# Gated delta rule in a two-layer decoder: the unit's output formed with features on partitions, its norm applied at the residual addition

## The reference, cut to what matters

```python
S = S * alpha_t; kv = k_t @ S; S = S + outer(k_t, (v_t - kv) * beta_t); o_t = q_t @ S
...
var = jnp.mean(jnp.square(o), axis=-1, keepdims=True)
o = o * lax.rsqrt(var + EPS) * norm_w
o = o * (z * jax.nn.sigmoid(z))
out = jnp.einsum('btv,hv->bth', o.reshape(b_, t_, VAL_DIM), out_w)
```

## Time and profile before

| | us |
|---|---|
| median of 3 runs | 1917.11 (1915.36 to 1921.35) |
| the profiled execution | 1916.25 |
| its span on the core | 1914.9 |
| PE busy | 1837.5 (96% of the span) |
| DVE busy | 1221.8 |
| POOL, ACT busy | 696.3, 681.2 |

### The profile page before, as it was taken

One profiled execution on the slowest core, in us unless ns is written; L12 is line 12 of the kernel. 1 busy time (PEld: TensorE's weight loads), 2 busy tenths in 40 slices (PEclk: granted clock), 3 DMA queues, 4 the chain that ended last, 5 costly groups with the idle time before them and its releaser, 6 DMA issues.

```text
span 1914.9 us, 39982 instructions
## 1 busy us (share of the span) xinstructions
PE 1837.5 (96%) x15048; PEld 1331.2 (70%) x15048; DVE 1221.8 (64%) x3371; ACT 681.2 (36%) x1755; POOL 696.3 (36%) x726
## 2 busy tenths in 40 slices
PE   7799999999899999999999999999999999999999
PEld 4466766776676666666445766666659979889698
DVE  6878888878766776777766766767655334234332
ACT  4223333333334555555000355565642211121211
POOL 4634443444215676666000166666634000000000
PEclk9889999999999999999999999999999999999999
DMA  5111101110103010010000000100030000000000
GB/s 186 29 22 21 31 15 28 23 25 14 23 15 124 25 37 25 26 37 20 1 1 1 10 20 20 29 20 20 20 144 34 1 10 1 10 1 1 10 1 10
DMA packets 94591, 52.22 MB, mean 27 GB/s; under 512 B 77256, under 2 KB 86336, under 8 KB 93632
## 3 DMA queue, kind: packets, MB, share of 16 engines
q1 hardware_dynamic: 94400, 49.65, 9.8%
HBM read 44.18 MB, written 5.45 MB: 26 GB/s over the span
## 4 chain that ended last, share of the span: by engine, by line
PE 68%; issue 2%; DVE 2%; ACT 1%; POOL 1%; DVEq 0%; ACTq 0%; POOLq 0%
PE ps L2534 18%; PE ps L1517 6%; PE ps L2406 5%; PE ps L2065 5%; PE ps L1539 5%; PE ps L1555 4%; PE ps L1594 4%; PE ps L1573 4%; PE ps L2612 3%; PE ps L1660 2%; PE ps L1526 2%; PE ps L1605 1%; PE ps L1581 1%; PE ps L1642 1%; PE ps L556 1%
## 5 line engine op out<-in xcount | busy, mean ns | idle before, releaser
L1978 POOL TENSOR_TENSOR h_w<-h_w 125x336 int32<-125x336 int32 x384 | 335.9, 904 | 210.8 <-ACT h_w L1759 210.7
L1863 DVE CUSTOM_DVE_ANT_0 h_w<-ps,h_w 112x375 f32<-112x375 f32 x512 | 263.4, 544 | 0.8 <-issue 0.5
L903 DVE SCALAR_TENSOR_TENSOR big_b<-ps,taps,big_b 128x444 f32<-128x444 f32 (+2 forms) x288 | 193.9, 673 | 34.3 <-ACT big_b L790 15.6
L1759 ACT ACTIVATE h_w<-ps 125x336 f32<-125x336 f32 x512 | 197.7, 468 | 21.7 <-PE ps L1539 21.7
L272 POOL TENSOR_TENSOR rstd<-var_eps,minus_half 112x4 f32<-112x4 f32 x12 | 12.2, 1015 | 408.0 <-DVE var_eps L259 408.0
L1539 PEld LDWEIGHTS ps<-h_w 32*125 32x125 f32 x3072 | 96.0, 183 | 62.3 <-issue 61.5
L1539 PE MATMUL ps<-h_w 32*125 32x112 f32 x3072 | 118.0, 282 | 8.0 <-DVE h_w L1863 5.6
L1872 DVE TENSOR_TENSOR h_w<-h_w,ps 128x112 f32<-128x112 f32 x128 | 34.7, 271 | 141.6 <-PE ps L1526 141.6
L1517 PE MATMUL ps<-h_w 32*112 32x375 f32 x1024 | 121.1, 519 | 0.8 <-DVE h_w L1863 0.8
L2065 PE MATMUL ps<-expert_w,big_a 128*112 128x512 f32 x256 | 114.1, 597 | 0.0
L556 PE MATMUL ps<-h_w,w 128*128 128x448 f32 x256 | 109.6, 552 | 4.6 <-ACT h_w L812 4.6
(11 more groups left out here) (357 smaller groups left out, 3852.7 us busy)
## 6 DMA issues: line engine op xcount, KB each, us to landing
h_w<-in_h SPq DMA_DIRECT2D x2, 4096.0 KB, 16.8
kq_w<-in_ctxT SPq DMA_DIRECT2D x16, 375.0 KB, 3.2
h_w<-in_ctxT SPq DMA_DIRECT2D x16, 375.0 KB, 3.3
h_w<-in_mask SPq DMA_DIRECT2D x16, 164.1 KB, 3.3
kq_w<-in_kq_w SPq DMA_DIRECT2D x8, 256.0 KB, 3.4
w<-in_vz_w SPq DMA_DIRECT2D x8, 256.0 KB, 3.5
blocks<-h_w SPq DMA_DIRECT2D x128, 12.2 KB
expert_w<-in_expert_w SPq DMA_DIRECT2D x1, 2048.0 KB
```

Source lines behind the costliest of these rows:

```text
L903: dve.scalar_tensor_tensor(p3(dst)[:, :, i:], p3(ps[:, bank, 0:GT])[:, :, 0:T - i], k.taps[:, h, n, TAPS - 1 - i:TAPS - i], p3(dst)[:, :, ...
L1759: act.activation(k.PTx[(4 * Q + r) % RING], ps[0:CK, turned_bank(Q, r), 0:NC * T], ACT.Exp).then_inc(s["exp"], 1)
L1863: dve.tensor_tensor_reduce(k.masked[r % 2], ps[0:T, score_bank(Q, r), 0:S2], k.mask_add[n % 2], -1.0, 3.0e38, ALU.add, ALU.min, k.neg_max[ ...
L1978: pool.tensor_tensor(P.bitcast(I32), P.bitcast(I32), k.mask_I[n % 2], ALU.mult).then_inc(s["weights"], 1)
```

## The change

O is formed transposed (features on partitions) by swapping the operands, so the transposes and their wait go. ACT squares all of it in one instruction; PE sums the squares of each token by four products of a 128x112 stationary operand with a single column that holds 1/128; ACT copies those means and adds 1e-6; POOL takes the power -1/2; DVE multiplies by norm weight and gate straight from bank 6; the root is applied in the addition to x, for which four instructions of 112x256 take the place of two of 112x512. Bank 6 is now released by the squares and by the gated product.

```diff
         elif slot == 3:                      # keys(): logG on PE
             if a > AHEAD:
-                pe.wait_ge(s["On"], a - AHEAD)
+                pe.wait_ge(s["squares"], a - AHEAD)
+                pe.wait_ge(s["gated"], a - AHEAD)
...
         if u:                                # out_of(u) on PE
-            pe.wait_ge(s["On"], u)
-        for j in range(G):
-            ins = pe.matmul(ps[0:T, 6, j * DK:(j + 1) * DK], k.R[u % 2][:, j, :], k.W0[u % 2][:, j * DK:(j + 1) * DK],
-                            start=True, stop=True)
+            pe.wait_ge(s["squares"], u)
+            pe.wait_ge(s["gated"], u)
+        for j, c in enumerate(PER_SEQ):
+            ins = pe.matmul(ps[:, 6, c], k.W0[u % 2][:, j * DK:(j + 1) * DK], k.R[u % 2][:, j, :], start=True, stop=True)
...
         if slot == 2:                        # tail(u, slot) on PE
-            pe.wait_ge(s["On"], u + 1)
-            pe.wait_ge(s["sz"], min(u + 2, UNITS))
-            if is_late(u):
+            pe.wait_ge(s["squares"], u + 1)
+            if u:
                 pe.wait_ge(s["gdn_x"], u)
-            for j in range(G):
-                ins = pe.transpose(ps[:, 4, j * T:(j + 1) * T], k.On[:, j * DK:(j + 1) * DK], k.ident[0:T, 0:T])
-            ins.then_inc(s["oT"], 1)
+            for j, c in enumerate(PER_SEQ):
+                ins = pe.matmul(ps[0:T, 0, j:j + 1], k.squared[:, c], k.mean_col[:, :], start=True, stop=True)
+            ins.then_inc(s["mean"], 1)
         elif slot == 4:
             pe.wait_ge(s["gated"], u + 1)
+            pe.wait_ge(s["o_var"], u + 1)
+            pe.wait_ge(s["sz"], min(u + 2, UNITS))
...
         keys(a, 2)                           # steady loop on PE
-        if u:
-            tail(u - 1, 2)
         solve(u, "Y2")
...
         keys(a, 10)
+        tail(u, 2)
         solve(u + 1, "M")
...
-        tail(u - 1, 2)                       # late loop on PE, behind V
+        if u > UNITS - AHEAD:
+            tail(u - 1, 2)
...
     def squares(u):                          # ACT
         act.wait_ge(s["O"], u + 1)
-        for j in range(G):
-            ins = act.activation(k.On[:, j * DK:(j + 1) * DK], ps[0:T, 6, j * DK:(j + 1) * DK], ACT.Square,
-                                 accum_out=k.var_eps[:, j:j + 1])
-        ins.then_inc(s["squares"], 1)
+        if u:
+            act.wait_ge(s["mean"], u)
+        act.activation(k.squared, ps[:, 6, 0:GT], ACT.Square).then_inc(s["squares"], 1)
+
+    def mean(u):
+        act.wait_ge(s["mean"], u + 1)
+        if u:
+            act.wait_ge(s["o_rstd"], u)
+        act.activation(k.var_eps[:, :], ps[0:T, 0, 0:G], ACT.Copy, bias=1e-6).then_inc(s["o_var"], 1)
...
         values(u + 1, 8)                     # steady loop on ACT
+        mean(u)
         solve(u + 1, "R")
...
         more = is_unit(u + 1)                # late loop on ACT
+        if u > UNITS - AHEAD:
+            mean(u - 1)
         solve(u, "A")
...
-        if slot == 1:                        # tail(u, slot) on DVE
-            dve.wait_ge(s["squares"], u + 1)
-            dve.tensor_scalar(k.var_eps[:, :], k.var_eps[:, :], 1.0 / DK, 1e-6, ALU.mult, ALU.add).then_inc(s["o_var"], 1)
-        elif slot == 2:
-            dve.wait_ge(s["o_rstd"], u + 1)
-            dve.tensor_tensor(four(k.On), four(ps[0:T, 6, 0:G * DK]), k.rstd[:, :].unsqueeze(2).to_broadcast([T, G, DK]),
-                              ALU.mult).then_inc(s["On"], 1)
-        elif slot == 3:
-            dve.wait_ge(s["oT"], u + 1)
+        if slot == 3:
+            dve.wait_ge(s["squares"], u + 1)
...
-            dve.scalar_tensor_tensor(k.oT, ps[:, 4, 0:GT], k.norm_w[:, 0:1], k.sz[u % 2], ALU.mult, ALU.mult).then_inc(s["gated"], 1)
+            dve.scalar_tensor_tensor(k.oT, ps[:, 6, 0:GT], k.norm_w[:, 0:1], k.sz[u % 2], ALU.mult, ALU.mult).then_inc(s["gated"], 1)
         elif slot == 5:
             dve.wait_ge(s["out"], u + 1)
-            for n in range(G // 2):
-                xs = k.x[:, g * G + 2 * n:g * G + 2 * n + 2, :]
-                ins = dve.tensor_tensor(xs, xs, two(ps[0:T, out_banks(u)[n], :]), ALU.add)
+            dve.wait_ge(s["o_rstd"], u + 1)
+            for j in range(G):
+                xs = k.x[:, g * G + j, :]
+                ins = dve.scalar_tensor_tensor(xs, ps[0:T, out_banks(u)[j // 2], (j % 2) * D:(j % 2 + 1) * D], k.rstd[:, j:j + 1], xs,
+                                               ALU.mult, ALU.add)
...
     def root(u):                             # POOL
         pool.wait_ge(s["o_var"], u + 1)
+        if u:
+            pool.wait_ge(s["gdn_x"], u)
...
             sums(u + AHEAD)                  # steady loop on POOL
-            root(u - 1)
...
             fades(u + AHEAD + 1)
+        root(u)
```

More of the change, by code:

```diff
@@ L50 @@
 zeros proj_kq tap_kq conv_kq proj_vz tap_v conv_v cum kk tanh sz logG gamma gam kq N0 QG vtok W0
-nd_w0 nd_w1 ni_in c_in tri td_w pair_in pair off_w dn_in0 dn_in1 M_ps M R_ps R Y1 A Y2 less Y3 R_sum O squares o_var o_rstd On oT gated out gdn_x
+nd_w0 nd_w1 ni_in c_in tri td_w pair_in pair off_w dn_in0 dn_in1 M_ps M R_ps R Y1 A Y2 less Y3 R_sum O squares mean o_var o_rstd gated out gdn_x
 ctx0 ctx1 mask_in0 mask_in1 k_bias
@@ L148, in memory @@
     k.W0 = [spare[:, n * G * DK:(n + 1) * G * DK] for n in range(2)]
-    k.On = k.xn[:, 0:2, :].rearrange("p a b -> p (a b)")
+    k.squared = k.silu[:, 0, :]
+    k.mean_col = sb("mean_col", [128, 1])
     k.beta_decay = k.small[:, 0:8, :].rearrange("p a b -> p (a b)").rearrange("p (n h g j) -> p n h g j", n=2, g=NG, j=G)
@@ L692, in gdn_pe @@
     pe.wait_ge(s["c_ident"], 16)
+    pe.wait_ge(s["setup_pool"], 2)
     start_pe_turn(pe, k, s, 0)
@@ L773, in gdn_pe @@
     cross_head_pe(pe, k, s, 0, 3)
-    for slot in range(4):
-        tail(UNITS - 1, slot)
+    tail(UNITS - 1, 2)
     cross_head_pe(pe, k, s, 0, 2)
-    for slot in (4, 5):
-        tail(UNITS - 1, slot)
+    tail(UNITS - 1, 4)
 def gdn_act(act, k, s):
@@ L891, in gdn_act @@
     act.wait_ge(s["const"], 64)
-    for part in (1, 0, 2, 3, 4):
+    cross_head_act(act, k, s, 0, 1)
+    mean(UNITS - 1)
+    for part in (0, 2, 3, 4):
         cross_head_act(act, k, s, 0, part)
@@ L960, in tail @@
         g = u % NG
-        if slot == 1:
+        if slot == 3:
             dve.wait_ge(s["squares"], u + 1)
-            dve.tensor_scalar(k.var_eps[:, :], k.var_eps[:, :], 1.0 / DK, 1e-6, ALU.mult, ALU.add).then_inc(s["o_var"], 1)
-        elif slot == 2:
-            dve.wait_ge(s["o_rstd"], u + 1)
-            dve.tensor_tensor(four(k.On), four(ps[0:T, 6, 0:G * DK]), k.rstd[:, :].unsqueeze(2).to_broadcast([T, G, DK]),
-                              ALU.mult).then_inc(s["On"], 1)
-        elif slot == 3:
-            dve.wait_ge(s["oT"], u + 1)
-            if u == 0:
+            if u:
+                dve.wait_ge(s["out"], u)
+            else:
                 dve.wait_ge(s["setup_dve"], 1)
-            dve.scalar_tensor_tensor(k.oT, ps[:, 4, 0:GT], k.norm_w[:, 0:1], k.sz[u % 2], ALU.mult, ALU.mult).then_inc(s["gated"], 1)
+            dve.scalar_tensor_tensor(k.oT, ps[:, 6, 0:GT], k.norm_w[:, 0:1], k.sz[u % 2], ALU.mult, ALU.mult).then_inc(s["gated"], 1)
         elif slot == 5:
             dve.wait_ge(s["out"], u + 1)
-            for n in range(G // 2):
-                xs = k.x[:, g * G + 2 * n:g * G + 2 * n + 2, :]
-                if u == UNITS - 1 and n == 1:
+            dve.wait_ge(s["o_rstd"], u + 1)
+            for j in range(G):
+                xs = k.x[:, g * G + j, :]
+                if u == UNITS - 1 and j == 2:
                     dve.wait_ge(s["out"], u + 2)
-                ins = dve.tensor_tensor(xs, xs, two(ps[0:T, out_banks(u)[n], :]), ALU.add)
+                ins = dve.scalar_tensor_tensor(xs, ps[0:T, out_banks(u)[j // 2], (j % 2) * D:(j % 2 + 1) * D], k.rstd[:, j:j + 1], xs,
+                                               ALU.mult, ALU.add)
             ins.then_inc(s["gdn_x"], 1)
@@ L1020, in gdn_dve @@
         h4, h3, h2 = head_due(u, 4), head_due(u, 3), head_due(u, 2)
-        if u:
-            tail(u - 1, 1)
-            tail(u - 1, 2)
         if h3 is not None:
@@ L1078, in gdn_dve @@
     cross_head_dve(dve, k, s, 0, 1)
-    for slot in range(6):
+    for slot in (3, 5):
         if slot == 5:
@@ L1153, in gdn_pool @@
             fades(u + AHEAD + 1)
+        root(u)
     for u in range(UNITS - AHEAD, UNITS):
         h3, h2 = head_due(u, 3), head_due(u, 2)
-        root(u - 1)
+        if u > UNITS - AHEAD:
+            root(u - 1)
         if h2 is not None:
@@ L2844, in gpsimd_program @@
     pool.memset(k.minus_half[:, :], -0.5).then_inc(s["setup_pool"], 1)
+    pool.memset(k.mean_col[:, :], 1.0 / DK).then_inc(s["setup_pool"], 1)
     pool.wait_ge(s["setup_pool"], 1)
```

## The result

The changed kernel takes 1927.01 us (median of 5 runs, 1922.21 to 1928.30), the kernel before 1916.71 (5 runs). The ratio is 1.005 with a 95% interval of 1.0033 to 1.0067: slower, by about 10 us, where 17.8 were forecast. The profiled execution took 1928.21 us, with a span of 1926.9.

The account below looks back on a forecast made before the run. PE was taken to bound 17 of 22 steady steps, DVE the other five; 21.6 - 1.8 - 1.0 + 3.3 - 0.9 - 3.4 = +17.8 us on 1916.25 gave 1934.1 us, range 1923 to 1944.

Parts of the forecast that it names:

- Term 4: In each PE-bound steady pass, logG waits for bank 6 until the gated product: 0.93 us, the largest term.
- One-column products: PE in steady passes: eight instructions for the mean's four products at 102 ns each, +0.82 us per pass.
- rival C: A product costs by its moving columns alone, 0.21 us for the eight instructions: +7 us, 1924; chance 6%.
- O transposed: O with swapped operands on PE: saved columns save nothing, taken as 0, between -0.1 and +0.1 us.
- Normal steps: 17 PE-bound steps of the steady loop: -0.48 + 0.82 + 0.93 = +1.27 us each, +21.6 us.
- rival B: Wait and sum as forecast, but the clock holds and single-column products cost 0.54 us: +4, 1920; chance 9%.
- The DVE steps: Five steady steps to u % 4 = 1, bounded by DVE: -0.36 us each, -1.8 us.
- The clock: PE at 1.2 GHz after passes with u % 4 = 1: count of four in six left as it is.
- The late loop: Y2 held behind the mean's copy +1.10, shorter squares -0.44: +0.66 per pass, +3.3; u = 24 -0.9, u = 26 -3.4.
- The end: Everything behind the delta rule was taken as unchanged.
- Rival A: The round trip through POOL and DVE was the bound and is gone, PE not held at logG: 1883; chance 5%.
- Rival D: Four additions take 0.6 us each, R_sum comes 0.3 us behind O, lower clock spreads: +17, 1951; chance 8%.

## Why the prediction was right, and where it was off

- **Direction and main mechanism: right.** Term 4 (bank 6) said 0.93 us before logG; the trace has 0.85 of idle, 0.94 from start to start, at K + 5.22 for 5.12. In the DVE passes the wait is 1.87 us where about 2.5 was forecast. The single wait on the kernel before gives 0.47 for 0.45. This is shown, not argued.
- **One-column products: right.** 0.82 from the row with 8 columns; 0.72 for the group and 0.07 more on M behind it. Doubling them costs 0.79 per pass. The rule of 25 ns (rival C) is out: it would be 0.2. The prediction names a table as this rule; the Trainium skill, TensorE: Matmul & The Clock Gate, section Back-to-back issue gap, says itself that its formula is for a product by itself and that in a stream of loads and products both set the spacing. The 90 ns measured per instruction side with that.
- **O transposed: right**, 0.88 from start to start both ways. **Normal steps: right**, +21.1 for +21.6. So rival B, which needed 0.54 for the products, is out.
- **The DVE steps: mis-sized.** The step "-1.88 + 0.64 + 0.88 = -0.36" measured -0.95, five times, 3 us in all. The additions cost 0.38 more, not 0.64: four in a row take 1.58. The row they were priced from was no match. Its two additions in the experts' layer go to the same part of x, and the kernel has the second wait for the first by a semaphore (`moe_x`); the four here go to different parts and wait for nothing. The larger part is the term I did not have: POOL's root, costed at nothing in its new place, moved POOL's sums out of the way of DVE's inversion rows (0.5 us a pass, shown by putting it back). Some 0.2 us of small terms go the other way.
- **The clock: mis-sized.** It was left as it was; four of six passes fell again, though not the same ones, and for 1.5 to 1.7 us each instead of 1.5 to 2.7. That four fell again is luck: the experiments had between one and six such passes in the steady loop, so this term moves the total by several us from kernel to kernel. The length of PE's wait does not order them: behind 1.87 us three of five fell in the changed kernel, behind 2.38 one of five with the root put back, behind 1.50 one of five with the old additions and none of five with the products doubled. How an edit bears on it stays open.
- **The late loop: mechanism right, size off.** V to Y2 grew by 0.90 (I had 1.10; ACT's two copies are only 0.07 apart from start to start), and the squares gave back 0.57 (I had 0.44): +0.31 per pass in u = 27 to 29 in place of +0.66. Of the two other passes with that forecast, u = 25 grew by 0.09, and from V of u = 30 to the last projection it is 0.06 less. u = 26 lost its wait and its half clock, -3.9 for -3.4. u = 24: -0.96 for -0.9. (All from V to V.)
- **The end: missed.** The prediction took everything behind the delta rule as unchanged, but the last unit's tail is mixed with the first attention: +1.6 us, half from the mask standing behind the root in POOL's list and half from the copies that stand behind the mean in ACT's.
- **Rival A: out.** All of PE's waits on L966 are gone, and the kernel is slower. **Rival D: out**; R_sum holds O only after the key-key product is moved, as its cover of 0.3 us suggests.

In all, 10.3 was measured for 17.8. By the table the errors are -0.4 (start), -0.5 (normal steps), -3.0 (DVE steps), -2.5 (clock), -3.0 (late loop) and +1.6 (end): the term that decides was hit, and the small ones happen to lie mostly on one side.

## What to carry to other kernels

Removing instructions from engines that are not the bound pays only in the passes where they are; look at what the edit does to the time at which a shared PSUM bank comes free, because the last reader may now stand behind other work in its engine's list. When such a wait appears, look for an instruction of the waiting engine whose inputs are ready and put it in front; then look at what that makes late (here R_sum), and do so only in the passes where it helps. A product with one moving column cost nearly as much here as one with 8 (90 and 102 ns an instruction), and half of it with 16-bit operands, so its element size matters more than its columns.

## What the hardware did that was not expected

- Halving the element size of a product's operands (128x112 stationary, one moving column) made the record of its load shorter (178 to 132 ns) and its spacing half (90 to 45 ns), besides halving the number of instructions: 0.72 to 0.18 us for the four products.
- A DVE product over 4 columns, with both inputs in SBUF, took 0.68 us beside a POOL instruction and 0.16 without it; one over a single column took 0.90 where it met one.
- Four additions with a factor, 112x256, take 0.39 us each in a row (1.58 for four), though each is listed with over 0.47; where the second of two had to wait for the first by a semaphore, the two took 0.92.
